# Graph layers: masks of the first stage written in place over the signs and stored twice per graph

## The chip, the cores and the metric

One core of a Trainium2 chip runs the whole kernel. The metric is the device time of one execution, in microseconds; lower is better. TensorE, VectorE (DVE in the rows), ScalarE (ACT), GpSimd (POOL) and SyncE (SP) each have their own queue of instructions, worked off in order, and are tied together by semaphores. All transfers are issued from SyncE's queue.

## What is computed

There are 16 graphs of 1024 nodes with 128 features and a dense weighted adjacency `adj` (about 6% of it not zero). Cut to what matters:

```python
h = relu(layernorm(x))
x = x + L0(h, adj)        # three times: h = h @ W + b; cos of the rows; (adj * cos) @ h
h = relu(layernorm(x))
keep = dilate(adj > 0)    # row by row, in order: removes neighbours by rank,
                          # each removal is made in row n and in column n
adj_d = adj * keep
x = x + L1(h, adj_d)      # three SAGE layers with batch norm over all 16 graphs,
                          # then a linear layer over the three outputs
```

`keep` depends on `adj` alone. For a graph it is the matrix R of what each row keeps, times its transpose: an edge stays where both ends keep it.

## The kernel before

The kernel has three stages: `layer0`, `layer1_middle` (twice over the graphs) and `layer1_last`. The change is in `layer0`, with its consequences for the loads of the mask in `layer1_middle`.

**Two programs in one stage.** `layer0` runs two things at once. The units (`plan_units`) are the 48 pairs of graph and layer of L0, with 16 steps each, 768 in all: TensorE makes a block of cosines (`cos`, lines 712 to 714), VectorE multiplies it by the adjacency into `ew` (line 895), and TensorE multiplies that by `Hr` (`agg`, line 721). `nh` and `nl` (lines 801 and 887) are the normed features at the beginning of a unit; the cosines of a unit can't begin before them. The dilation (`plan_dilation`) works on quads of four graphs, two quads at a time, block by block of 128 rows (k = 0 to 7). For a block, the rows of `adj` are loaded (`row`, three buffers `af`), ScalarE writes their signs into `Ab` as fp8 (line 815), a DMA transpose brings them into the slab `TT` (`fill`), VectorE strikes what earlier blocks removed (`low`, lines 911 and 915), GpSimd masks a triangle (line 641) for VectorE's `cross` (line 925), and rounds of `rank`, `rule` and `drop` follow. Then TensorE, ScalarE (`v`, line 832) and VectorE (`wide`, line 1010) write the kept row block into `TT`. `check` compares the last two rounds and reads the diagonal block in `TT`.

**The slab.** `TT[slot, m, k, x, s]` holds for one graph column block 2m + s and row block k, the two columns of a pair beside each other, one byte each. There are eight slots: quads 0 and 1, then quads 2 and 3 in the same ones.

**Masks.** When enough row blocks are done, a flip (m, j), a DMA transpose of column pair m and row blocks 4j to 4j + 3, is put into one of four flip buffers. With it VectorE makes `mask(q, j)` (line 1022) for row blocks q = 2m and 2m + 1: half a row block, 128 x 512 bytes, R times its transpose. It goes to one of three buffers `kp`, and from there SyncE stores it in `S["keep"]` (line 618), 64 KB each, 256 in all. Before the next mask can use the buffer, VectorE waits for the semaphore `kps` of that store. Flips (0,0) and (1,0) can go from k = 3, (2,0) from k = 5, and (3,0), (0,1), (1,1), (2,1), (3,1) from k = 7: 2, 1 and 5 for each graph. They are ordered by (m, j), and within it by graph.

**The order.** A planner in Python (`Planner.order`) lays all steps of both programs out beforehand, by list scheduling with fixed costs and ranks (a lower rank goes first among steps ready at the same time: `cos` 0, `mask` 3, `wide` 4, `low` and `cross` 5, `check` 6). Each engine then runs its list in that order, whatever really happens. Rings of buffers (`kp` 3, `flip` 4, `af` 3, `v` 3) are part of the plan. An issue on SyncE is counted as 70 ns, a flip's transfer as 600 ns, a mask's store as 300, and 100 ns for a signal between engines.

**Later stages.** `layer1_middle` loads the mask of a graph, 1 MB, as 8 rows of 1 KB for each partition, and multiplies the adjacency by it in eight instructions of 128 x 1024: all on VectorE in the first pass (line 1632), half on VectorE (line 1713) and half on GpSimd (line 1735) in the second.

Of the kernel before, what the change touches and what calls it, by code (L numbers as in the profile page):

```python
# [17 lines left out]
G = 16  # L18
N = 1024
D = 128  # L20
NK = 8
BANK = 76
# [13 lines left out]
RANKS = 3 * NK + 2  # L36
FLIPS = [(0, 0), (1, 0), (2, 0), (3, 0), (0, 1), (1, 1), (2, 1), (3, 1)]
# [20 lines left out]
def flat2(t):  # L58
    return t[:].rearrange("p k d -> p (k d)")

# [44 lines left out]
def build(nc, A):  # L105
    with ExitStack() as top:
# [17 lines left out]
        S["keep"] = nc.dram_tensor("scr_keep", [G, NK, 128, N], U8, kind="Internal").ap()  # L124
# [5 lines left out]
        C["kp0"] = C["stage"][:, 0:4, :].rearrange("p a b -> p (a b)").bitcast(FP8).rearrange("p (k n) -> p k n", k=NK)  # L130
# [173 lines left out]
def readers(quad, i, k):  # L304
    seen = [(q, k // 4) for q in range(NK)] + [(k, 1 - k // 4)]
    return [("dve", "mask", quad, i, q, j) for q, j in seen]
# [94 lines left out]
def plan_dilation(P):  # L401
# [3 lines left out]
    for n in sorted(range(QUADS * NK), key=lambda n: (n // NK // 2 * NK + n % NK, n // NK % 2)):  # L405
# [7 lines left out]
        for i in range(Q):  # L413
            freed = readers(quad - 2, i, k) if quad > 1 else []
# [42 lines left out]
def layer0_plan():  # L457
# [10 lines left out]
               [("dma", "mask", quad, i, q, j) for q in range(NK) for j in range(2)] + [("act", "row", n, i, j) for n in range(NK * QUADS) for i in range(Q) for j in range(2)])  # L468
    return P.order({"D0": 1, "D1": 1, "af": 3, "v": 3, "kp": 3, "flip": 4}), P.turns["kp"]


def layer0(nc, A, C, S):
    with ExitStack() as ctx:
# [3 lines left out]
        T = P.sems("at0 at1 fl0 fl1 fl2 fl3 af0 af1 af2 sign low au x bs b0 b1 ct ru vr sd again v8 wb wd av rw kp kps0 kps1 kps2 sum tot flag")  # L477
# [29 lines left out]
        kp = [P.sb(f"kp{i}", [128, 512], FP8) for i in range(3)]  # L507
# [6 lines left out]
        plan, ring = layer0_plan()  # L514
# [22 lines left out]
        def in_pairs(half_row):  # L537
            return half_row.rearrange("p (m x s) -> p m s x", m=2, s=2)

        def as_blocks(half_row):  # L540
            return half_row.rearrange("p (m s x) -> p m s x", m=2, s=2)

# [9 lines left out]
        every = [("dve", "mask") + a for a in ring]  # L552
# [8 lines left out]
        def sp(e):  # L561
# [3 lines left out]
            for kind, *a in plan["sp"]:  # L565
# [24 lines left out]
                elif kind == "fill":  # L590
# [4 lines left out]
                    if quad > 1:  # L595
                        wait_masks(e, readers(quad - 2, i, k))
                    e.dma_start_transpose(TT[:, slot, :, k].rearrange("p m x s -> p m (x s)").bitcast(F16),
                                          Ab[:, slot, :].bitcast(F16)).then_inc(T[f"at{quad % 2}"], 16)
                elif kind == "flip":
                    quad, i, m, j = a  # L600
                    r = nth["sp", "flip", quad, i, m, j] - 1
                    e.wait_ge(T["rw"], max(nth["dve", "wide", quad * NK + b, i, m // 2] for b in range(4 * j, 4 * j + 4)))
                    if r > 3:
                        wait_masks(e, users_of(*of["sp", "flip"][r - 4]))
# [1466 lines left out]
```

## Time and profile before

| | us |
|---|---|
| median of 3 runs | 2692.42 |
| lowest and highest | 2684.85 and 2693.45 |
| the profiled execution, its own time | 2686.08 |
| its span, first to last instruction | 2684.3 |
| TensorE busy | 2574.4 |
| VectorE busy | 2082.9 |
| ScalarE busy | 1365.9 |
| GpSimd busy | 598.8 |

The times below are from the start of the span of the profiled execution, which is 1.8 us shorter than its time. In it the first stage takes some 1630 us. A busy time of TensorE is that of instructions in flight: matmuls overlap, and their ends are modelled. "Idle before" is the time in which an engine had nothing to run, put down to what released it.

### The profile page before, as it was taken

What the parts mean: (1) busy time and instruction counts of PE and PEld (TensorE: products, weight loads), DVE (VectorE), ACT (ScalarE), POOL (GpSimd) and SP (SyncE); (2) the same over time, 40 slices, a digit from 0 to 9 for tenths busy, and PEclk for the clock granted to TensorE, in tenths of its full rate; (3) what the DMA queues carried; (4) which work ended last, traced back from release to release, by engine and by line L of the source; (5) the groups of instructions that cost most, each with busy time, mean ns of one, the idle gap of its engine ahead of it and who ended that gap; (6) DMA issues with size and microseconds to landing.
All of it is one profiled execution on the core that took longest, in us unless ns stands there. A gap on an engine that the chain in (4) does not pass through costs nothing. (4 is left out here: it accounts for less than half of the span.)

```text
span 2684.3 us, 38830 instructions
## 1 busy us (share of the span) xinstructions
PE 2574.4 (96%) x12390; PEld 1634.7 (61%) x12390; DVE 2082.9 (78%) x5413; ACT 1365.9 (51%) x4060; POOL 598.8 (22%) x265
## 2 busy tenths in 40 slices
PE   6999989999989999999999998999999999999898
PEld 4666656656655666656665664555555555555797
DVE  5788889889889988989989877766666635666676
ACT  4566645665654676646663421332322344443676
POOL 0000000000000000000000003766666603433673
PEclk8999999999999999999999999999999999999999
DMA  7254184364177347157345223555555419996663
GB/s 246 79 164 132 48 201 136 97 158 155 43 197 194 89 146 192 49 157 198 93 113 159 46 69 137 201 192 192 192 191 191 183 55 387 405 404 261 251 234 152
DMA packets 325878, 455.48 MB, mean 170 GB/s; under 512 B 155680, under 2 KB 218528, under 8 KB 325664
## 3 DMA queue, kind: packets, MB, share of 16 engines
q1 hardware_dynamic: 325664, 452.89, 52.4%
q8 instruction: 102, 1.67, 0.3%
q14 instruction: 112, 0.92, 0.1%
HBM read 352.13 MB, written 67.11 MB: 156 GB/s over the span
## 5 line engine op out<-in xcount | busy, mean ns | idle before, releaser
L721 PE MATMUL a_acc<-a_ew,a_Hr 128*128 128x512 f32 x1536 | 754.4, 600 | 0.0
L895 DVE TENSOR_TENSOR a_ew<-adj,a_cos 128x512 f32<-128x512 f32 x768 | 508.0, 681 | 69.0 <-PE a_cos L714 67.1
L712 PE MATMUL a_cos<-a_nh 128*128 128x512 f32 x768 | 417.2, 543 | 31.5 <-DVE a_ew L895 16.4
L721 PEld LDWEIGHTS a_acc<-a_ew,a_Hr 128*128 128x128 f32 x1536 | 275.8, 190 | 153.7 <-issue 110.2
L641 POOL TENSOR_TENSOR a_Au<-a_Ab,tri 128x512 fp8e4<-128x512 fp8e4 x32 | 36.8, 1150 | 1367.2 <-ACT a_Ab L815 1367.2
L832 ACT ACTIVATE a_v<-a_D,a_wb,a_small 128x256 f16<-128x256 f32 x512 | 287.2, 632 | 99.8 <-PE a_D L754 59.9
L714 PE MATMUL a_cos<-a_nh,a_nl 128*128 128x512 f32 x768 | 305.5, 398 | 0.0
L713 PE MATMUL a_cos<-a_nl,a_nh 128*128 128x512 f32 x768 | 302.9, 394 | 0.0
L822 ACT ACTIVATE a_vr<-a_D,a_small 128x128 f16<-128x128 f32 x432 | 161.9, 457 | 134.1 <-DVE a_small L967 133.8
L1387 PE MATMUL b_acc<-adj,b_z 128*128 128x512 f32 x512 | 225.0, 592 | 0.0
L712 PEld LDWEIGHTS a_cos<-a_nh 128*128 128x128 f32 x768 | 146.1, 190 | 127.5 <-DVE a_ew L895 52.7
L1484 PE MATMUL b_acc<-adj,b_z 128*128 128x512 f32 x512 | 222.5, 592 | 0.0
L1724 POOL TENSOR_TENSOR b_dsum<-adj 128x1024 f32<-128x1024 f32 x15 | 133.3, 8886 | 387.8 <-DVE adj L1632 387.8
L1728 POOL TENSOR_TENSOR b_dsum<-b_dsum,adj 128x1024 f32<-128x1024 f32 x90 | 211.5, 2350 | 12.9
L1022 DVE TENSOR_TENSOR a_kp<-a_T,stage 128x512 fp8e4<-128x512 fp8e4 x256 | 171.5, 688 | 47.2 <-DMA scr_keep<-a_kp 42.3
L815 ACT ACTIVATE a_Ab<-stage 128x512 fp8e4<-128x512 f32 x256 | 155.8, 630 | 99.7 <-DMA stage<-in_adj 98.9
L1010 DVE SCALAR_TENSOR_TENSOR a_T<-a_v,a_Ab 128x512 fp8e4<-128x512 f16 x256 | 173.1, 686 | 28.6 <-ACT a_v L832 28.2
L713 PEld LDWEIGHTS a_cos<-a_nl,a_nh 128*128 128x128 f32 x768 | 147.0, 191 | 64.3 <-issue 51.7
L714 PEld LDWEIGHTS a_cos<-a_nh,a_nl 128*128 128x128 f32 x768 | 145.4, 189 | 33.9
L1484 PEld LDWEIGHTS b_acc<-adj,b_z 128*128 128x128 f32 x512 | 96.0, 190 | 114.3 <-issue 112.2
L1387 PEld LDWEIGHTS b_acc<-adj,b_z 128*128 128x128 f32 x512 | 94.8, 190 | 107.1 <-issue 107.1
L784 ACT ACTIVATE h<-a_Hr 128x128 f32<-128x128 f32 x384 | 113.1, 297 | 78.3 <-DVE a_Hr L875 78.2
(267 smaller groups left out, 4361.3 us busy)
## 6 DMA issues: line engine op xcount, KB each, us to landing
adj<-in_adjT SPq DMA_DIRECT2D x108, 1024.0 KB, 12.6
adj<-in_adjT SPq DMA_DIRECT2D x128, 512.0 KB, 4.0
stage<-in_adj SPq DMA_DIRECT2D x256, 256.0 KB, 3.3
scr_keep<-a_kp SPq DMA_DIRECT2D x256, 64.0 KB, 1.8
scr_z<-b_zT SPq DMA_DIRECT2D x32, 512.0 KB, 3.7
scr_ag<-b_a SPq DMA_DIRECT2D x32, 512.0 KB, 3.3
stage<-scr_keep SPq DMA_DIRECT2D x13, 1024.0 KB, 7.3
b_kp<-scr_keep SPq DMA_DIRECT2D x12, 1024.0 KB, 7.8
```

Source lines behind the costliest of these rows:

```text
L712: e.matmul(cos[j][:], n[:, blk(k)], n[:, half(j)], start=True, stop=False)
L713: e.matmul(cos[j][:], n[:, blk(k)], m[:, half(j)], start=False, stop=False)
L714: e.matmul(cos[j][:], m[:, blk(k)], n[:, half(j)], start=False, stop=True).then_inc(E["cos"], 1)
L721: e.matmul(acc[j][:], Hr[u % 2][:, k, :], ew[idx % EW][:], start=(k == 0), stop=(k == NK - 1)).then_inc(E["agg"], 1)
L822: e.activation(vr[p][:, i, :], D0[:, i, :], ACT.Abs, bias=sm[p]["b2"][:, i:i + 1], scale=sm[p]["sc"][:, i:i + 1]).then_inc(T["vr"], 1)
L832: t = e.activation(v[c % 3][:, g * 256:g * 256 + 256].rearrange("p (x s) -> p s x", s=2), D1[:, 2 * g:2 * g + 2, :], ACT.Abs, bias=wb[p][: ...
L895: e.tensor_tensor(ew[idx % EW][:], adj[g % 2][:, k, half(j)], cos[j][:], ALU.mult).then_inc(E["ew"], 1)
L1010: e.scalar_tensor_tensor(TT[:, slot, 2 * j:2 * j + 2, k].rearrange("p m x s -> p m (x s)"), v[c % 3][:].rearrange("p (m c) -> p m c", m=2) ...
L1022: e.tensor_tensor(as_blocks(kp[c % 3][:]), row_half(slot, j, q), turned[:, :, :, :, q % 2], ALU.mult, saturate=False).then_inc(T["kp"], 1)
L1387: t = e.matmul(acc[j][:], src[:, q, :], adj[n % 3][:, q, half(j)], start=(q == 0), stop=(q == NK - 1))
L1484: t = e.matmul(acc[j][:], z[m % 2][:, q, :], adj[slot(m)][:, q, half(j)], start=(q == 0), stop=(q == NK - 1))
L1728: e.tensor_tensor(d, d, b[:, q, :], ALU.add).then_inc(E["ds"], 1)
```

## The change

The mask is written over R itself, in `TT`, instead of into a ring of `kp` buffers. When all 16 masks of a graph are made, its slab is stored by two transfers of 512 KB, in the slab's own layout, so 32 stores instead of 256. `S["keep"]` is now `[G, 128, NK * N]`; later stages load it as one piece of 8 KB for each partition and read it with steps that undo the layout (`masked`). `dilate_all`, which runs only when a check fails, writes the same layout.

Since masks overwrite what flips and `check` read, there are new waits. A mask (q, j) waits for all flips that read its block, as far as they are released by then (`flips_ahead`); a flip waits for masks already made in the blocks that it reads (`masks_ahead`); the mask that holds the diagonal block waits for `check` of its row block. A fill of quads 2 and 3 waits for both stores of the graph that had the slot. The order of the flips is changed: all of one graph, then the next graph. The constant `MASK` is 3, the rank that masks had before.

```diff
+def released(m, j):
+    return max(2 * m + 1, 4 * j + 3)
+def crossing(q, j):
+    return [(m, q // 4) for m in (2 * j, 2 * j + 1)]
+def flips_ahead(q, j):
+    return [f for f in crossing(q, j) if released(*f) <= released(q // 2, j)]
+def masks_ahead(m, j):
+    return [(q, h) for q in range(NK) for h in range(2)
+            if (m, j) in crossing(q, h) and released(q // 2, h) < released(m, j)]
 ...
-            freed = readers(quad - 2, i, k) if quad > 1 else []
+            freed = [("dma", "store", quad - 2, i, j) for j in range(2)] if quad > 1 else []
 ...
-        for m, j in FLIPS:
-            if k == max(2 * m + 1, 4 * j + 3):
-                for i in graphs_of(quad):
+        for i in graphs_of(quad):
+            for m, j in FLIPS:
+                if k == released(m, j):
                     transfer(("flip", quad, i, m, j), 600, [("dve", "wide", quad * NK + b, i, m // 2)
-                             for b in range(4 * j, 4 * j + 4)], "flip", "flip", rank=2)
+                             for b in range(4 * j, 4 * j + 4)] + [("dve", "mask", quad, i) + a for a in masks_ahead(m, j)],
+                             "flip", "flip", rank=2)
+            for m, j in FLIPS:
+                if k == released(m, j):
                     for q in (2 * m, 2 * m + 1):
                         last = ("flip", ("flip", quad, i, m, j)) if q % 2 else None
-                        add("dve", ("mask", quad, i, q, j), 605, 3, [("dma", "flip", quad, i, m, j),
-                            ("dve", "wide", quad * NK + q, i, j)], f"flip{quad}{i}{m}{j}", "kp", last)
-                        transfer(("mask", quad, i, q, j), 300, [("dve", "mask", quad, i, q, j)], None, None, "kp")
+                        add("dve", ("mask", quad, i, q, j), 605, MASK, [("dma", "flip", quad, i, m, j),
+                            ("dve", "wide", quad * NK + q, i, j)] + ([("dve", "check", quad * NK + q)] if j == q // 4 else [])
+                            + [("dma", "flip", quad, i) + f for f in flips_ahead(q, j)], f"flip{quad}{i}{m}{j}", None, last)
+            if k == NK - 1:
+                for j in range(2):
+                    transfer(("store", quad, i, j), 1400, [("dve", "mask", quad, i, q, j) for q in range(NK)])
 ...
                     if quad > 1:
-                        wait_masks(e, readers(quad - 2, i, k))
+                        e.wait_ge(T[f"st{i}"], 32 * (quad - 1))
 ...
-                elif kind == "mask":
-                    quad, i, q, j = a
-                    c = ring[quad, i, q, j]
-                    wait_masks(e, [("dve", "mask", quad, i, q, j)])
-                    e.dma_start(S["keep"][quad * Q + i, q][:, half(j)], kp[c % 3][:].bitcast(U8)).then_inc(
-                        T[f"kps{c % 3}"], 16)
+                elif kind == "store":
+                    quad, i, j = a
+                    slot = Q * (quad % 2) + i
+                    wait_masks(e, [("dve", "mask", quad, i, q, j) for q in range(NK)])
+                    if quad and j == 0:
+                        e.wait_ge(T[f"st{i}"], 32 * quad)
+                    e.dma_start(S["keep"][quad * Q + i][:, 4096 * j:4096 * j + 4096],
+                                TT[:, slot, 2 * j:2 * j + 2].rearrange("p m k x s -> p (m k x s)").bitcast(U8)).then_inc(
+                        T[f"st{i}"], 16)
 ...
-                    if c > 2:
-                        e.wait_ge(T[f"kps{c % 3}"], 16 * (c // 3))
+                    if j == q // 4:
+                        e.wait_ge(T["v8"], nth["dve", "check", quad * NK + q])
+                    mine = row_half(slot, j, q)
                     turned = flip[r % 4].bitcast(FP8).rearrange("p (m t) (x s) -> p m t x s", t=2, s=2)
-                    e.tensor_tensor(as_blocks(kp[c % 3][:]), row_half(slot, j, q), turned[:, :, :, :, q % 2], ALU.mult,
-                                    saturate=False).then_inc(T["kp"], 1)
+                    e.tensor_tensor(mine, mine, turned[:, :, :, :, q % 2], ALU.mult, saturate=False).then_inc(T["kp"], 1)
 ...
+        def masked(b, c, q):
+            row = b[:, q, :].rearrange("p (m s x) -> p m s x", s=2, x=128)
+            return row, row, c.rearrange("p (m k x s) -> p m k s x", m=4, k=NK, s=2)[:, :, q]
 ...
-                e.dma_start(kp[n % 2].bitcast(U8), S["keep"][ORDER[n]].rearrange("k p n -> p k n")).then_inc(
+                e.dma_start(kp[n % 2].bitcast(U8), S["keep"][ORDER[n]]).then_inc(
 ...
-                    e.tensor_tensor(b[:, q, :], b[:, q, :], c[:, q, :], ALU.mult).then_inc(E["mk"], 1)
+                    e.tensor_tensor(*masked(b, c, q), ALU.mult).then_inc(E["mk"], 1)
```

## Rows read from the trace of the kernel before

**Rows 1.** The page, part 1: busy time, share and instructions of each engine.

```profile
PE 2574.4 (96%) x12390; PEld 1634.7 (61%) x12390; DVE 2082.9 (78%) x5413; ACT 1365.9 (51%) x4060; POOL 598.8 (22%) x265
```

**Rows 2.** Stretches: length, PE, PEld, DVE, ACT, POOL busy, clock, DMA; two sums.

```profile
60.00:340.00 280.00, 277.65 (x1467) 180.87 (x1467) 227.61 (x655) 180.30 (x502) 6.59 (x6) 1.00 0.37 106
...
sum 1560.00, PE 1503.13 PEld 962.33 DVE 1356.98 ACT 898.63 POOL 34.60; mean PE 107.37 PEld 68.74 DVE 96.93 ACT 64.19 POOL 2.47
...
720.00:900.00 180.00, 164.70 (x801) 102.17 (x799) 162.65 (x379) 97.42 (x259) 4.79 (x4) 1.00 0.70 174
...
sum 540.00, PE 495.33 PEld 312.14 DVE 478.96 ACT 254.39 POOL 12.80; mean PE 82.56 PEld 52.02 DVE 79.83 ACT 42.40 POOL 2.13
...
1700.00:1800.00 100.00, 100.00 (x377) 56.09 (x376) 64.12 (x147) 30.74 (x98) 69.89 (x22) 1.00 0.52 194
```

**Rows 3.** Stretches of L895 (two), of L1022 (sum of the six); L1022's durations, first and last.

```profile
60.00:340.00 280.00, 92.50 (x138) 1.00 0.37 106
...
720.00:900.00 180.00, 52.70 (x82) 1.00 0.70 174
...
sum 540.00, DVE 140.42; mean DVE 23.40
...
L1022 DVE TENSOR_TENSOR a_kp<-a_T,stage x256: 636/685/1418, 335.0 to 1573.3; 128x512 fp8e4<-128x512 fp8e4 x128
```

**Rows 4.** Waits of the first stage: engine, line, what released it; total, times, longest.

```profile
PE a_cos L712 <- DVE a_nl L887: 12.4, 9, 3.0
PE a_D L754 <- ACT a_v L832: 11.5, 14, 2.3
...
ACT a_Ab L815 <- DMA stage<-in_adj: 98.9, 67, 5.9
DVE a_kp L1022 <- DMA scr_keep<-a_kp: 42.3, 49, 2.3
DVE a_kp L1022 <- DMA stage<-a_T: 1.8, 1, 1.8
```

**Rows 5.** The same waits from 720 to 900 us alone.

```profile
ACT a_Ab L815 <- DMA stage<-in_adj: 24.3, 14, 4.0
DVE a_kp L1022 <- DMA scr_keep<-a_kp: 15.6, 19, 2.1
```

**Rows 6.** Timeline: start, duration, instruction; a mask that waits for a store.

```profile
740.29 1.19 SPq L597 DMA_TRANSPOSE a_T<-a_Ab  x1
...
741.52 0.59 SPq L618 DMA_DIRECT2D scr_keep<-a_kp  x1
...
742.93 0.69 DVE L1022 TENSOR_TENSOR a_kp<-a_T,stage 128x512 fp8e4<-128x512 fp8e4 x1 [2.15 <-DMA scr_keep<-a_kp]
```

**Rows 7.** Timeline: a late row, and TensorE's wait 5 us after.

```profile
1067.63 0.63 ACT L815 ACTIVATE a_Ab<-stage 128x512 fp8e4<-128x512 f32 x1 [2.75 <-DMA stage<-in_adj]
...
1072.62 0.80 PE L712 MATMUL a_cos<-a_nh 128*128 128x512 f32 x1 [3.03 <-DVE a_nl L887]
```

**Rows 8.** Store issues (ns, min/median/max); transfers: KB each, median us to landing.

```profile
L618 SPq DMA_DIRECT2D scr_keep<-a_kp x256: 332/431/1826, 335.8 to 1574.0; - x128
...
stage<-scr_keep SPq DMA_DIRECT2D x13, 1024.0 KB, 7.3
...
scr_x<-xt SPq DMA_DIRECT2D x16, 512.0 KB, 2.7
...
stage<-a_T SPq DMA_TRANSPOSE x128, 2.5
```

**Rows 9.** Groups by form: count, busy us, mean ns, idle before: mask, `low`, triangle, later products.

```profile
L1022 DVE TENSOR_TENSOR a_kp<-a_T,stage 128x512 fp8e4<-128x512 fp8e4 x256 | 171.5, 688 | 47.2 <-DMA scr_keep<-a_kp 42.3 <-DMA stage<-a_T 1.8
...
L641 POOL TENSOR_TENSOR a_Au<-a_Ab,tri 128x512 fp8e4<-128x512 fp8e4 x32 | 36.8, 1150 | 1367.2 <-ACT a_Ab L815 1367.2
...
L1735 POOL TENSOR_TENSOR adj<-adj,stage 128x1024 f32<-128x1024 f32 x20 | 39.6, 2012 | 121.4 <-DMA adj<-in_adjT 121.4
...
L911 DVE TENSOR_TENSOR a_T<-a_T 128x512 fp8e4<-128x512 fp8e4 x32 | 22.1, 694 | 0.0
```

More of the change, by code:

```diff
@@ L21 @@
 NK = 8
-BANK = 76
+BANK = 77
 MAGIC = 8388608.0
@@ L467, in layer0_plan @@
                                        for i in range(Q) for q in range(NK) for j in range(2)] +
-               [("dma", "mask", quad, i, q, j) for q in range(NK) for j in range(2)] + [("act", "row", n, i, j) for n in range(NK * QUADS) for i in range(Q) for j in range(2)])
-    return P.order({"D0": 1, "D1": 1, "af": 3, "v": 3, "kp": 3, "flip": 4}), P.turns["kp"]
+               [("dma", "store", quad, i, j) for j in range(2)] + [("act", "row", n, i, j) for n in range(NK * QUADS) for i in range(Q) for j in range(2)])
+    return P.order({"D0": 1, "D1": 1, "af": 3, "v": 3, "flip": 4})
 def layer0(nc, A, C, S):
@@ L476, in layer0 @@
                    "bst bag lnsd lnrs lnr " + " ".join(f"adj{i}{k}" for i in range(2) for k in range(NK)))
-        T = P.sems("at0 at1 fl0 fl1 fl2 fl3 af0 af1 af2 sign low au x bs b0 b1 ct ru vr sd again v8 wb wd av rw kp kps0 kps1 kps2 sum tot flag")
+        T = P.sems("at0 at1 fl0 fl1 fl2 fl3 af0 af1 af2 sign low au x bs b0 b1 ct ru vr sd again v8 wb wd av rw kp st0 st1 st2 st3 sum tot flag")
         W, rows = P.sb("W", [128, 3, 128]), P.sb("rows", [128, 3, 128])
@@ L513, in layer0 @@
         mv4 = C["mv"][:].rearrange("p (g k) -> p g k", k=NK)
-        plan, ring = layer0_plan()
+        plan = layer0_plan()
         nth = {}
@@ L550, in users_of @@
             return [("dve", "mask", quad, i, q, j) for q in (2 * m, 2 * m + 1)]
-        every = [("dve", "mask") + a for a in ring]
+        every = [("dve", "mask") + a for a in of["dve", "mask"]]
         def earlier(engine, kind, upto):
@@ L602, in sp @@
                     e.wait_ge(T["rw"], max(nth["dve", "wide", quad * NK + b, i, m // 2] for b in range(4 * j, 4 * j + 4)))
+                    ahead = [("dve", "mask", quad, i) + a for a in masks_ahead(m, j)]
                     if r > 3:
-                        wait_masks(e, users_of(*of["sp", "flip"][r - 4]))
+                        ahead += users_of(*of["sp", "flip"][r - 4])
+                    if ahead:
+                        wait_masks(e, ahead)
                     e.dma_start_transpose(flip[r % 4], TT[:, Q * (quad % 2) + i, m, 4 * j:4 * j + 4].rearrange(
@@ L623, in sp @@
                     wait_masks(e, every)
-                    stored = [ring[quad, i, q, j] for q in range(NK) for j in range(2)]
-                    for c in range(3):
-                        e.wait_ge(T[f"kps{c}"], max(16 * (m // 3 + 1) for m in stored if m % 3 == c))
-                    e.dma_start(C["kp0"].bitcast(U8), S["keep"][ORDER[0]].rearrange("k p n -> p k n")).then_inc(
-                        C["kpload"], 16)
+                    e.wait_ge(T[f"st{i}"], 32 * (quad + 1))
+                    e.dma_start(C["kp0"].bitcast(U8), S["keep"][ORDER[0]]).then_inc(C["kpload"], 16)
             e.wait_ge(E["xs"], 16 * (G - 1))
-            for c in range(3):
-                e.wait_ge(T[f"kps{c}"], 16 * ((2 * G * NK + 2 - c) // 3))
+            for i in range(Q):
+                e.wait_ge(T[f"st{i}"], 32 * QUADS)
         def pool(e):
@@ L1193, in dve @@
                         e.wait_ge(E["tr"], j + 1)
[L1194 to L1195 removed]
+                        for m in range(2):
+                            into = kp[:, 512 * j + 256 * m:512 * j + 256 * m + 256].rearrange("p (x s) -> p s x", s=2)
+                            turned = Dp[:, j, 256 * m:256 * m + 256].rearrange("p (s x) -> p s x", s=2)
+                            mine = R[:, q, 512 * j + 256 * m:512 * j + 256 * m + 256].rearrange("p (s x) -> p s x", s=2)
+                            t = e.scalar_tensor_tensor(into, turned, 0.5, mine, ALU.is_lt, ALU.is_gt, saturate=False)
+                        t.then_inc(E["kp"], 1)
                 def sp(e):
                     e.wait_ge(E["kp"], 2)
[L1199 to L1200 removed]
+                    e.dma_start(graph(S["keep"]).rearrange("o p (m k c) -> (o p) m k c", k=NK, c=256)[:, :, q],
+                                kp[:].bitcast(U8).rearrange("p (m c) -> p m c", c=256)).then_inc(E["load"], 16)
                     e.wait_ge(E["load"], 16)
```

37 lines of the change are left out of this document (15 added, 22 removed).

## The prediction

> **What bounds the kernel now.** I read the page first, for the shares. TensorE is busy 96% of the span, and VectorE in places nearly as much [rows 1]. Such a share doesn't say whether TensorE waits, so next came the busy times by stretch. The first stage ends near 1630 us. From 60 to 1620 us TensorE is idle 57 us in all (1560 less the 1503.13 of the first sum line), and this idle time isn't spread evenly [rows 2]. Six stretches, 340 to 440, 720 to 900, 1040 to 1080, 1140 to 1180, 1400 to 1480 and 1480 to 1580, hold 540 less 495.33 = 44.7 us of it (the second sum line), and 140.42 us of the mask products, at 688 ns each some 205 of the 256, lie in them [rows 3, 9]. The largest, 720 to 900, has 15.3 us. The 280 us from 60 to 340, without masks, have 2.3.
>
> The second measure is the pace of the `ew` product, one for each of the 768 steps of the first stage: 138 in 280 us from 60 to 340, 82 in 180 us from 720 to 900 [rows 3], so 2.03 against 2.20 us for a step. TensorE's work, not VectorE, is therefore the floor, and what can be won is idle time in the mask stretches.
>
> What ends the idle time is in the waits [rows 4]. VectorE waits 42.3 us for `kps`, the landing of a mask's store from the ring of three buffers. TensorE's own waits are for `ew`, for `nl` (12.4 us), and for ScalarE's `v` (11.5 us). ScalarE waits 98.9 us for the rows that SyncE loads. In 720 to 900 alone these are 15.6 us (VectorE, stores) and 24.3 us (ScalarE, rows) [rows 5]. The timeline shows how they hang together [rows 6]: the mask of 742.93 was kept back 2.15 us, and the store whose buffer it needed went out only at 741.52, since SyncE was busy with the transpose of 740.29. SyncE's queue is full in such places, with transposes of 1.19 us and stores of 0.59 us. The planner that wrote the order counts 70 ns for each issue, so it can't see this. Further on, the chain reaches TensorE [rows 7]: a row late by 2.75 us, then the triangle product, VectorE's `cross` and, behind it in the queue, `nl`, and TensorE starts the next unit after 3.03 us of idleness.
>
> **The change, part by part.** *Stores.* 256 stores of 64 KB become 32 of 512 KB. Each issue takes a median of 431 ns [rows 8], so SyncE is relieved of 224 x 0.431 = 97 us, nearly all in the mask stretches. The bytes stay the same. VectorE's ring wait goes: 42.3 us [rows 4], nearly all in the six stretches and 15.6 of it in the longest [rows 5]. What is late next is the flip transpose, below.
>
> *The mask itself* writes bytes two apart instead of side by side. The trace has the same size written this way, in place: 694 ns for `low` against 688 for the mask [rows 9]. 256 x 6 ns = 1.5 us. Two more waits stand ahead of some masks, on semaphores mostly long reached; back-to-back instructions with three waits already follow each other without idle time, so I take nothing, at most 1.5 us.
>
> *The flips.* Before, a mask needed one flip. Now it also needs those that read the blocks it overwrites. At k = 7 a graph has five flips and ten masks; the first mask (6,0) needs flips (3,0), (0,1), (1,1), and the masks of (2,1) need (3,1). The fifth flip takes the ring slot of the first, so it waits for (7,0). One flip takes SyncE 1.19 us, and lands 2.5 us after its issue [rows 8]. Between the graphs: the next graph's third flip gets its slot when (5,1) of this graph is done. Only masks (6,1) and (7,1), 1.2 to 1.4 us, and one or two `ew` products of about 0.6 us stand between, against 2.5 to 3.7 us for issue and landing. Left over are 0 to 2.5 us; I take 1.5, for 16 graphs 24 us. The bounds: nothing, if VectorE has dilation work planned there (then the latency hides behind it), and 16 x 3.7 = 59 us if nothing covers it. At k = 3 and k = 5 at most two flips are needed and they go out together; included in that. What queues behind a waiting mask is `ew`, so this is the very place where the 42.3 us hurt. Behind a waiting flip on SyncE stand row loads and fills; but before, 256 stores waited there for masks in the same way, and now 32 do, so the queue is freer on balance.
>
> *Fills.* A fill of graphs 8 to 15 now waits for both stores of the graph two quads before. The nearest row, a 512 KB store to scratch, lands in 2.7 us [rows 8]. Two in a row, before the first fill of two quads: 0 to 6 us for each quad, on the chain of the dilation, not on TensorE. The last mask starts at 1573 [rows 3] and the stage ends near 1630, so up to 50 us of such delay is covered by the last units; without that cover it would cost its full 12 us. By the Trainium skill ("DMA: Bandwidth & Descriptors", Anatomy of one DMA) a transfer costs about 2.0 us plus its bytes at 436 GB/s, an estimate of 3.2 us for such a store; the trace has 2.7, and either is covered.
>
> *Later stages.* The loads of the masks keep their 1 MB, in pieces of 8 KB instead of 1 KB. They land in 7.3 us now [rows 8], and nobody waits for them: TensorE is busy 100% from 1700 on [rows 2]. VectorE's and GpSimd's mask products now read bytes two apart. For VectorE the 694 against 688 says nothing changes. GpSimd takes 2012 ns; the nearest row is the triangle product, which reads bytes two apart: 1150 ns for 512 [rows 9], so up to 2.3 us for 1024, 4 x 0.3 us for a graph. In that stage GpSimd waits for the loads of the adjacency itself, so its work has room; I take nothing, and at most 3 us, for the last graph and its neighbours. By the Trainium skill ("GPSIMD Engine Reference", Performance pitfalls for Q7 kernels) reads slow by half from a step above 8 bytes. The step here is 2, so by the rule GpSimd's time stays; no run yet shows it.
>
> **The sum.** VectorE's idle time changes by -42.3 + 24 + 1.5 = -17 us. What a microsecond of it is worth to TensorE: in the six stretches 44.7 us of idleness stand beside 42.3 us of ring waits, but part of it comes from late rows. I take 0.6, so -10 us. The freed SyncE brings rows earlier: of its 57 us TensorE waits 11.5 for `v` and 12.4 for `nl` [rows 4], which hang on ScalarE and so on the rows; I take a quarter of these 24, -6 us. Sum: -16 us. The static order, which the planner shuffles with every edit, can add or take some microseconds; I give it no sign. The profiled execution took 2686.08 us; 2670 would follow from it. The median of the runs shown, 2692.42, is 6.3 above it, so the runs give 2676.
>
> **Rivals.** (a) *The flips take the place of the stores.* The wait for each graph is 3.7 us, uncovered: 59 us in place of 42.3, plus 1.5. VectorE idles 18 us more, at the worth of 0.6 TensorE loses 11 us, and the freed SyncE does not help, since it waits itself: 2703. It decides against the change from 42.3 / 16 = 2.6 us of waiting per graph on. For it: the planner counts 770 ns (70 for the issue, 600 for the transfer, 100 for the signal) for what takes 2.5 to 3.7, and at k = 7 the masks come one every 2 us. Against it: in the trace only one wait of 1.8 us was for a flip [rows 4]. The Trainium skill has the rule behind it ("DMA: Bandwidth & Descriptors", Rules for kernel authors): issue a DMA early and wait late; three flips ahead of a mask instead of one brings the wait nearer. (b) *Nothing shows.* The ring wait was slack of VectorE, TensorE's idleness comes from the coupling of units and dilation, and the new order keeps it: 2692, 2684 to 2700. For it: in the wait at 742.93 TensorE had matmuls to do. (c) *All of it comes back.* Flips are covered and SyncE was the cause of nearly all: -41 us of TensorE's 44.7, 2650. For it: only 2.3 us of idleness in the 280 us without masks.
>
> **How the numbers follow.** Forecast 0.45, (c) 0.15, (b) 0.22, (a) 0.18. Within 0.3% is +-8 us, about what this measurement can tell from no change. The forecast's own range is 2665 to 2684; nine tenths of it and all of (c) are faster, (b) is mostly same. Faster 0.59, same 0.22, slower 0.19. The range that holds 8 in 10 reaches from 2652, close to (c), to 2703, where (a) stands.
>
> **What the profile would show.** Right: no wait of a mask for a store; the mask product still near 690 ns; 32 stores; in the mask stretches TensorE idle 25 us instead of 45; waits of masks for flips of 10 to 40 us, most at k = 7; ScalarE's wait for rows below 80 us; from 1700 on no difference. Wrong: flip waits above 42 us, or TensorE's idle time unmoved though VectorE's ring waits are gone, or the last mask later than the end of the units.

## The result, and the profile after

| us | before | after |
|---|---|---|
| median of 4 runs | 2690.78 | 2657.26 |
| lowest and highest | 2684.85 and 2693.45 | 2653.77 and 2661.80 |
| the profiled execution, its own time | 2686.08 | 2658.54 |
| its span | 2684.3 | 2656.7 |

The ratio is 0.9879, with a 95% interval of 0.9856 to 0.9903: the kernel is 33.5 us faster, twice the 16 us of the forecast. The page after, part 1:

```profile
PE 2568.9 (97%) x12390; PEld 1636.7 (62%) x12390; DVE 2079.9 (78%) x5413; ACT 1365.2 (51%) x4060; POOL 606.5 (23%) x265
```

The counts are those of [rows 1], and the busy times nearly so. What went is idle time, and it went in the first stage: the last `agg` of the units, and the first instruction of the middle stage (a constant `onesf` that VectorE writes), before and then after, by tile (duration min/median/max, first and last start):

```profile
L721 PE MATMUL a_acc<-a_ew,a_Hr x1536: 590/592/1057, 34.1 to 1620.3; 128*128 128x512 f32 x192
...
L1648 DVE MEMSET onesf<- x1: 165/165/165, 1630.0 to 1630.0; 128x128 f32 x1
```

```profile
L745 PE MATMUL a_acc<-a_ew,a_Hr x1536: 590/592/1057, 34.1 to 1590.8; 128*128 128x512 f32 x192
...
L1680 DVE MEMSET onesf<- x1: 165/165/165, 1600.5 to 1600.5; 128x128 f32 x1
```

The first stage is 29.5 us shorter. The stages behind it take 1.9 us more (2656.7 - 1600.5 = 1056.2 against 2684.3 - 1630.0 = 1054.3). So the two profiled executions differ by 27.6 us, and the medians by 33.5: the profiled execution before lies 4.7 us under its median, that after 1.3 us above. In which stage the other 5.9 us lie, no trace shows. The stretches of the kernel after, with that of the `ew` product (line 919) in 720 to 900 and the sum of the prediction's six mask stretches:

```profile
60.00:340.00 280.00, 277.08 (x1463) 180.08 (x1464) 226.85 (x654) 179.54 (x499) 6.73 (x6) 1.00 0.36 106
340.00:440.00 100.00, 94.26 (x461) 60.92 (x460) 92.18 (x240) 45.72 (x124) 2.20 (x2) 0.98 0.64 182
720.00:900.00 180.00, 169.64 (x829) 107.42 (x828) 160.73 (x362) 87.78 (x253) 5.37 (x4) 1.00 0.73 191
...
720.00:900.00 180.00, 56.24 (x86) 1.00 0.73 191
...
sum 540.00, PE 521.35 PEld 332.88 DVE 486.64 ACT 263.86 POOL 7.57; mean PE 86.89 PEld 55.48 DVE 81.11 ACT 43.98 POOL 1.26
...
60.00:1590.00 1530.00, 1494.98 (x7540) 961.24 (x7541) 1349.59 (x3655) 897.65 (x2500) 35.96 (x30) 1.00 0.45 129
```

Up to the end of the units TensorE is now idle 1530 - 1494.98 = 35.0 us, 22 less than the 57 of [rows 2]. Without masks, 60 to 340, nothing changed (2.9 against 2.3 us). In 720 to 900 idleness fell from 15.3 to 10.4 us, and 86 `ew` products run there instead of the 82 of [rows 3]. The six stretches together have 540 - 521.35 = 18.7 us of it, and 188 of the 256 masks lie in them. The other 7.6 us of the 29.5 are not in TensorE's idle column; matmuls in flight overlap, so this column need not hold all of its waiting.

The waits of the first stage: TensorE's for `ew` before, which [rows 4] leaves out, and then those after, which answer to [rows 4]:

```profile
PE a_cos L712 <- DVE a_ew L895: 16.4, 16, 2.1
```

```profile
ACT a_Ab L839 <- DMA stage<-in_adj: 88.4, 61, 8.1
...
PE a_D L778 <- ACT a_v L856: 11.8, 17, 1.9
...
DVE a_T L1048 <- issue: 10.8, 7, 3.5
...
DVE a_T L1048 <- DMA stage<-a_T: 7.0, 6, 1.5
PE a_cos L736 <- DVE a_nl L911: 6.4, 6, 2.4
PE a_cos L736 <- DVE a_ew L919: 5.8, 8, 1.3
```

The wait for stores is gone. Masks wait 17.8 us for flips: 7.0 us by name, and 10.8 put down to "issue", where no semaphore event of the profile ends the wait. TensorE's wait for `ew` fell from 16.4 to 5.8. Its wait for `nl` fell from 14.8 to 6.4, both counted from the stage's start (the 12.4 of [rows 4] leave out the first 60 us, and without these it is 4.0 after). That for `v` is as it was. ScalarE's wait for rows fell only from 98.9 to 88.4. The products by form, and the transfers of the page:

```profile
L1048 DVE TENSOR_TENSOR a_T<-a_T,stage 128x512 fp8e4<-128x512 fp8e4 x256 | 168.1, 692 | 19.7 <-issue 10.8 <-DMA stage<-a_T 7.0 <-DVE a_X L1028 0.9
L1767 POOL TENSOR_TENSOR adj<-adj,stage 128x1024 f32<-128x1024 f32 x20 | 42.0, 2132 | 121.1 <-DMA adj<-in_adjT 121.1
```

```profile
scr_keep<-a_T SPq DMA_DIRECT2D x32, 512.0 KB, 3.2
...
stage<-scr_keep SPq DMA_DIRECT2D x13, 1024.0 KB, 6.8
```

A mask takes 692 ns against 688 [rows 9]; there are 32 stores, and the loads of the later stages land no later than in [rows 8].

### The profile page after: what moved, and what is told of

The parts are those of the page before. It is cut to its first block and busy times, and to the rows that moved or that the text cites. A ratio compares the mean times of both kernels' runs of the same rounds, so it can differ in the third digit from the quotient of the medians.

```text
span 2656.7 us, 38841 instructions
## 1 busy us (share of the span) xinstructions
PE 2568.9 (97%) x12390; PEld 1636.7 (62%) x12390; DVE 2079.9 (78%) x5413; ACT 1365.2 (51%) x4060; POOL 606.5 (23%) x265
## 5 line engine op out<-in xcount | busy, mean ns | idle before, releaser
L736 PE MATMUL a_cos<-a_nh 128*128 128x512 f32 x768 | 421.2, 548 | 12.4 <-DVE a_nl L911 6.4
L839 ACT ACTIVATE a_Ab<-stage 128x512 fp8e4<-128x512 f32 x256 | 155.8, 631 | 88.7 <-DMA stage<-in_adj 88.4
L1048 DVE TENSOR_TENSOR a_T<-a_T,stage 128x512 fp8e4<-128x512 fp8e4 x256 | 168.1, 692 | 19.7 <-issue 10.8
## 6 DMA issues: line engine op xcount, KB each, us to landing
adj<-in_adjT SPq DMA_DIRECT2D x108, 1024.0 KB, 12.7
```

Source lines behind the costliest of these rows:

```text
L736: e.matmul(cos[j][:], n[:, blk(k)], n[:, half(j)], start=True, stop=False)
L1048: e.tensor_tensor(mine, mine, turned[:, :, :, :, q % 2], ALU.mult, saturate=False).then_inc(T["kp"], 1)
```

## The experiments

Three questions: is it the stores on SyncE, the ring wait, or the planner's new order? And how much does an order change the time by itself? Every kernel's profile was read at the same four places, and the table has them, each from that kernel's own profiled execution: the last mask's start (the end of the dilation), the last `agg`'s start (the end of the units), the start of the middle stage, and TensorE's wait there for the first masked block of the adjacency. "Before" is the median of the kernel before on the same chip. Runs with different medians of it were on different chips or at different times; differences between them, taken below from the medians, shift by up to 3 us if they are taken from the ratios.

| kernel | median | before | ratio, 95% | last mask | last agg | middle | wait |
|---|---|---|---|---|---|---|---|
| before | 2690.78 | | | 1573.3 | 1620.3 | 1630.0 | 8.7 |
| after | 2657.26 | 2690.78 | 0.9879, 0.9856 to 0.9903 | 1556.1 | 1590.8 | 1600.5 | 8.6 |
| e1 extra stores | 2689.32 | 2690.71 | 0.9995, 0.9985 to 1.0004 | 1587.4 | 1621.4 | 1631.0 | 8.5 |
| e2 with ring wait | 2733.09 | 2690.71 | 1.0166, 1.0137 to 1.0195 | 1630.5 | 1665.6 | 1675.2 | 8.6 |
| e3 before, by graph | 2691.88 | 2690.71 | 1.0003, 0.9992 to 1.0014 | 1625.3 | 1621.0 | 1634.5 | 12.4 |
| e4 old plan | 2675.31 | 2690.71 | 0.9936, 0.9918 to 0.9955 | 1606.6 | 1583.1 | 1615.8 | 31.6 |
| e5 tiny stores | 2687.61 | 2693.36 | 0.9982, 0.9971 to 0.9993 | 1586.2 | 1620.2 | 1629.9 | 8.7 |
| e6 no wait | 2689.04 | 2693.36 | 0.9987, 0.9978 to 0.9997 | 1587.3 | 1621.3 | 1630.9 | 8.5 |
| e7 old plan, stores | 2705.54 | 2693.36 | 1.0057, 1.0036 to 1.0078 | 1631.3 | 1601.0 | 1641.1 | 39.0 |
| e8 and ring wait | 2730.53 | 2693.36 | 1.0148, 1.0127 to 1.0168 | 1658.7 | 1621.7 | 1668.7 | 45.9 |
| e9 masks aside | 2670.55 | 2691.36 | 0.9934, 0.9918 to 0.9951 | 1573.7 | 1600.7 | 1610.3 | 8.5 |
| e10 aside, e8's rest | 2703.01 | 2691.36 | 1.0045, 1.0029 to 1.0062 | 1634.9 | 1627.0 | 1644.9 | 16.9 |
| e11 true costs | 2637.83 | 2691.36 | 0.9806, 0.9790 to 0.9822 | 1568.0 | 1562.0 | 1577.5 | 14.5 |
| e12 rows on ScalarE | 2662.10 | 2691.36 | 0.9888, 0.9871 to 0.9904 | 1562.0 | 1596.7 | 1606.3 | 8.5 |
| e13 before, signal | 2680.48 | 2693.22 | 0.9961, 0.9950 to 0.9971 | 1615.9 | 1611.1 | 1624.8 | 12.6 |
| e14 after, signal | 2687.27 | 2693.22 | 0.9981, 0.9970 to 0.9992 | 1619.2 | 1593.0 | 1628.8 | 34.6 |
| e15 before, true costs | 2655.19 | 2693.22 | 0.9867, 0.9847 to 0.9887 | 1561.4 | 1588.1 | 1597.8 | 8.6 |
| e16 e11, MASK 4 | 2649.79 | 2693.22 | 0.9853, 0.9834 to 0.9871 | 1581.8 | 1564.3 | 1591.0 | 25.6 |
| e17 before, both | 2640.47 | 2691.63 | 0.9797, 0.9774 to 0.9820 | 1575.5 | 1576.3 | 1585.9 | 8.5 |
| e18 after, both | 2671.15 | 2691.63 | 0.9918, 0.9898 to 0.9939 | 1601.0 | 1563.0 | 1610.3 | 46.2 |

In every row the middle stage begins some 9.7 us after the last `agg`, or 9 to 10 us after the last mask, whichever is later. So two chains end the stage, and the two columns say which of them did. In ten of the kernels (e3, e4, e7, e8, e10, e11, e13, e14, e16, e18) it was the dilation, and TensorE waits 12 to 46 us for the first block there, where it waits some 8.6 us otherwise.

**e1, e2 and e3: the stores and the ring wait, put back one by one; the order of the flips alone.** e1 keeps the instructions of after on all other engines and adds 256 stores of 64 KB of a constant on SyncE, each behind its mask; e2 adds a mask's wait for the store three masks ago.

```diff
+    timed = [(P.steps[("sp",) + name].begin, 0, name) for name in out["sp"]]
+    timed += [(s.end, 1, ("extra",) + s.name[1:]) for key, s in P.steps.items() if key[:2] == ("dve", "mask")]
+    out["sp"] = [name for _, _, name in sorted(timed, key=lambda t: t[:2])]
...
+                elif kind == "extra":
+                    wait_masks(e, [("dve", "mask", quad, i, q, j)])
+                    e.dma_start(S["dump"][quad * Q + i, q][:, half(j)], C["UL"][:].bitcast(U8)[:, 0:512]).then_inc(
+                        T[f"dump{c % 3}"], 16)
```

(Left out: the scratch tensor, three semaphores and the room for them, and a wait for all extra stores at the end of the stage.) Ahead of the mask, in e2 alone:

```diff
+                    if c > 2:
+                        e.wait_ge(T[f"dump{c % 3}"], 16 * (c // 3))
```

e3 is the kernel before with the loops over flips turned:

```diff
-        for m, j in FLIPS:
-            if k == max(2 * m + 1, 4 * j + 3):
-                for i in graphs_of(quad):
+        for i in graphs_of(quad):
+            for m, j in FLIPS:
+                if k == max(2 * m + 1, 4 * j + 3):
```

> The changed kernel with 256 more stores of 64 KB on SyncE, one behind each mask and waiting for it, of a constant to an unused scratch tensor; nobody waits for them before the end of the stage. Theory 1 (the gain of 33 us came from VectorE's ring wait): SyncE's 97 us of issues are slack, the time stays within 5 us of the changed kernel, 2652 to 2662. Theory 2 (it came from the freed queue of SyncE): 15 us or more come back, 2672 or above. Theory 3 (it came from the new order): no change, as in theory 1.

> As the run before, and each mask also waits for the landing of the extra store three masks ago, so the ring wait is back. Theory 1: 20 to 33 us above the run before, which means near 2685. Theory 2: at most 8 us above it. Theory 3: both runs stay below 2670, since the order of the changed kernel is kept.

> The kernel before with nothing changed but the order of flips and masks: all of one graph, then the next. Theory 1 and theory 2: the ring and the 256 stores are still there, so 2685 to 2700. Theory 3: below 2675.

e1 gives back 32.1 us, nearly all of the gain. e2 costs 43.8 us more, which none of the three theories had foretold, so the two together (76) are more than twice what the change brought. The order of the flips alone brings nothing. The extra stores of e1, and its waits of masks and rows:

```profile
L656 SPq DMA_DIRECT2D scr_dump<-UL x256: 319/430/1879, 338.8 to 1588.1; - x128
```

```profile
ACT a_Ab L852 <- DMA stage<-in_adj: 109.6, 58, 8.3
...
DVE a_T L1061 <- issue: 23.0, 12, 6.4
PE a_cos L749 <- DVE a_ew L932: 21.1, 23, 2.8
DVE a_T L1061 <- DMA stage<-a_T: 17.8, 13, 2.5
```

An issue takes 430 ns. Masks wait 40.8 us for flips in place of 17.8, and behind a waiting mask stands `ew`: TensorE waits 21.1 us for it, 5.8 in after. From 60 to 1621 us it is idle 57.6 us in e1, against 35.0 to the end of the units in after. SyncE's queue around 738 us in e1, and then in after, by timeline (start, duration, instruction):

```profile
736.12 1.05 SPq L656 DMA_DIRECT2D scr_dump<-UL  x2
737.28 1.19 SPq L634 DMA_TRANSPOSE stage<-a_T  x1
738.51 0.58 SPq L649 DMA_DIRECT2D scr_keep<-a_T  x1
739.13 1.86 SPq L656 DMA_DIRECT2D scr_dump<-UL  x3
741.47 1.19 SPq L623 DMA_TRANSPOSE a_T<-a_Ab  x1
742.71 0.58 SPq L656 DMA_DIRECT2D scr_dump<-UL  x1
743.38 2.50 SPq L634 DMA_TRANSPOSE stage<-a_T  x2
```

```profile
732.55 0.57 SPq L644 DMA_DIRECT2D scr_keep<-a_T  x1
735.46 1.19 SPq L618 DMA_TRANSPOSE a_T<-a_Ab  x1
737.17 2.51 SPq L629 DMA_TRANSPOSE stage<-a_T  x2
739.73 0.57 SPq L644 DMA_DIRECT2D scr_keep<-a_T  x1
```

In e1 the queue is free for 0.8 of these 9.8 us (the largest gap, 740.99 to 741.47, is 0.5 us), and a flip (L634) that is ready has to stand in line. In after, where the stores are missing, it is free for 2.9 of 7.7 us, with one gap of 2.3 us (733.12 to 735.46). No mask waits just here. The longest wait of one in e1 comes 50 us later; SyncE's queue, VectorE's and TensorE's, in order:

```profile
777.41 1.19 SPq L623 DMA_TRANSPOSE a_T<-a_Ab  x1
...
779.27 0.90 SPq L656 DMA_DIRECT2D scr_dump<-UL  x2
...
780.75 0.46 SPq L656 DMA_DIRECT2D scr_dump<-UL  x1
781.30 2.50 SPq L634 DMA_TRANSPOSE stage<-a_T  x2
...
786.22 1.30 DVE L1061 TENSOR_TENSOR a_T<-a_T,stage 128x512 fp8e4<-128x512 fp8e4 x2 [6.44 <-issue]
...
789.29 0.50 PE L749 MATMUL a_cos<-a_nh 128*128 128x512 f32 x1 [2.78 <-DVE a_ew L932]
```

SyncE issues without a break from 777.41 on, and the last of the two flips leaves its queue at 783.80. The mask starts 2.4 us after that, with `nl` and `ew` behind it, and TensorE stands still for 2.78 us. That this flip is what the mask waited for fits the 2.5 us of [rows 8], but the trace names no releaser.

The ring wait of e2, in a plan that doesn't know of it, is twice that of [rows 4], and costs half of its length:

```profile
DVE a_T L1064 <- DMA scr_dump<-UL: 84.0, 48, 5.2
```

**e4, e7 and e8: the old resources in the plan.** In e4 the planner still counts 256 stores and the ring of three, though neither exists; e7 issues the stores where they are planned (e1's), e8 adds the ring wait of e2.

```diff
-    + [("dma", "flip", quad, i) + f for f in flips_ahead(q, j)], f"flip{quad}{i}{m}{j}", None, last)
+    + [("dma", "flip", quad, i) + f for f in flips_ahead(q, j)], f"flip{quad}{i}{m}{j}", "kp", last)
+    transfer(("planned", quad, i, q, j), 300, [("dve", "mask", quad, i, q, j)], None, None, ("kp", ("mask", quad, i, q, j)))
...
-    return P.order({"D0": 1, "D1": 1, "af": 3, "v": 3, "flip": 4})
+    return P.order({"D0": 1, "D1": 1, "af": 3, "v": 3, "kp": 3, "flip": 4})
```

> The changed kernel, laid out by a planner that still counts 256 stores and a ring of three buffers for the masks; nothing of them is issued, so VectorE waits for no store and SyncE has 32 stores. Theories 1 and 2: within 8 us of the changed kernel, 2649 to 2665. Theory 3, in the form that a plan without the ring packs the work better: 15 us or more above it, 2672 or more.

> The changed kernel laid out for 256 stores and a ring of three (as in the fourth experiment), and now the 256 stores are really issued where the plan has them, of a constant; no mask waits for one. Theory 2 (SyncE's issues cost wherever they are): 15 to 30 us above the fourth experiment, 2690 to 2705. Theory 2 with a plan that has room for them: 2675 to 2682.

> As the run before, and each mask waits for the landing of the store three masks ago, as before the change. Theory 1 (the ring wait is worth 0.6 us of TensorE a us, 25 us): 2710 to 2730. Theory 2 alone (where SyncE is full the ring wait adds nothing of its own): within 8 us of the run before. In the first plan the ring added 44 us, with 84 us of waits; here the plan spaces the masks for the ring, so waits of 40 to 50 us are expected.

e4 has only 15.4 us of the gain. In it the units end 7.7 us earlier than in after, but the dilation ends 50 us later, and TensorE waits for it:

```profile
PE b_acc L1420 <- DVE adj L1665: 32.3, 2, 31.6
```

In this plan the stores cost 30.2 us again (e7 less e4, on two chips; 33 by the ratios), and the ring wait 25.0. So the price of the stores hardly depends on the plan in these two, while that of the ring wait does: with the ring in the plan masks wait 53.9 us for stores instead of 84.0. e8 has stores and ring wait again, and is still 37 us slower than the kernel before.

**e5 and e6: what of a store costs.** e5 is e1 with 8 bytes for each partition in place of 512; e6 is e1 without the stores' wait for masks.

```diff
-   e.dma_start(S["dump"][quad * Q + i, q][:, half(j)], C["UL"][:].bitcast(U8)[:, 0:512]).then_inc(
+   e.dma_start(S["dump"][quad * Q + i, q][:, 512 * j:512 * j + 8], C["UL"][:].bitcast(U8)[:, 0:8]).then_inc(
```

```diff
-   wait_masks(e, [("dve", "mask", quad, i, q, j)])
```

> The changed kernel with 256 extra stores as in the first experiment (SyncE, one behind each mask, waiting for it), but of 8 bytes per partition, 1 KB in all instead of 64. Theory 2a (the issue on SyncE costs): the time is that of the first experiment, 2685 to 2693. Theory 2b (the bytes on the DMA engines cost): it is that of the changed kernel, 2652 to 2664.

> The same 256 stores of 64 KB at the same places of SyncE's list, not waiting for the masks. Theory 2a (issue time on SyncE, about 110 us of it): 2680 or above. Theory 2c (each store ties SyncE to VectorE, so that it can't run ahead with rows and transposes): below 2668.

Neither the bytes nor the waiting: by the ratios e5 is 0.13% below e1 and e6 0.08%, at most 3.5 us of the 32. The issues of e5 take what those of e1 took:

```profile
L656 SPq DMA_DIRECT2D scr_dump<-UL x256: 319/430/1840, 338.7 to 1586.9; - x128
```

256 x 0.43 = 110 us of SyncE's time in its crowded stretches cost some 30 us.

**e9 and e10: masks not in place.** The masks go to three side buffers, and the waits that writing in place needs leave the code and the plan, that for `check` too. The 32 stores take the slab without masks, so these two kernels leave the masks out of what later stages read. e10 has this with the plan, the stores and the ring wait of e8.

```diff
-    for b in range(4 * j, 4 * j + 4)] + [("dve", "mask", quad, i) + a for a in masks_ahead(m, j)],
+    for b in range(4 * j, 4 * j + 4)],
...
-    e.tensor_tensor(mine, mine, turned[:, :, :, :, q % 2], ALU.mult, saturate=False).then_inc(T["kp"], 1)
+    e.tensor_tensor(as_blocks(side[(nth["dve", "mask", quad, i, q, j] - 1) % 3][:]), mine, turned[:, :, :, :, q % 2], ALU.mult, saturate=False).then_inc(T["kp"], 1)
```

> The changed kernel with the masks written beside the slab, into three small buffers that nobody stores; the 32 stores take the slab as it is, without masks. So the extra waits of in-place writing (masks for the flips that read their block, masks for check, flips for earlier masks) go from the code and from the plan; stores, their number and the fills' wait for them stay. Theory 4 (in-place writing has a price of its own, which the gain of 33 us is already net of): 10 to 35 us below the changed kernel, 2622 to 2647. Rival: the waits are covered, within 8 us of it, 2649 to 2665.

> The plan, the 256 extra stores and the ring wait of the eighth experiment, but masks beside the slab as in the run before. This is nearly the kernel before, with 32 stores more. Theory 4: 25 us or more below the eighth experiment, 2690 to 2705. Rival: what lies between the eighth experiment and the kernel before (39 us) is the 32 stores and the fills that wait for them, and it stays at 2720 to 2735.

e9 has fewer constraints and is 13 us slower than after; e10 is 27.5 us faster than e8, as the theory of a price of in-place writing had it. The same edit has either sign. My theory that the waits of the in-place masks are a cost which the gain has to pay fell in e9 for the written plan. Since a mask's median duration is the same there (685 ns), I put the 13 us down to the plan, which is an argument and was not tested by itself.

**e11 and e12: act on the cause.** e11 lets the planner count what an issue on SyncE takes; e12 takes the 256 row loads from SyncE's queue and issues them from ScalarE's, in the order of after's plan.

```diff
-        self.add("sp", name, 70, rank, after, chain, takes)
+        self.add("sp", name, 1200 if name[0] in ("fill", "flip") else 500, rank, after, chain, takes)
```

```diff
+    timed = [(P.steps[("act",) + name].begin, 1, name) for name in out["act"]]
+    timed += [(P.steps[("sp",) + name].begin, 0, ("load",) + name[1:]) for name in out["sp"] if name[0] == "row"]
+    out["act"] = [name for _, _, name in sorted(timed, key=lambda t: t[:2])]
+    out["sp"] = [name for name in out["sp"] if name[0] != "row"]
```

> The changed kernel, with a planner that counts an issue on SyncE as 1200 ns for a transpose and 500 ns for any other transfer, in place of 70. Theory 2 (SyncE's issue time is the hidden resource, and the list is laid out in ignorance of it): 5 to 20 us below the changed kernel, 2637 to 2652. Rival: the list on each engine is already near enough, within 5 us.

> The changed kernel, with the 256 loads of rows of the adjacency issued from ScalarE's queue instead of SyncE's, at the places that the plan gives them. Theory 2: SyncE is freed of another 110 us or more of issues; if its queue still limits the mask stretches, 5 to 20 us below the changed kernel, if it doesn't any more, no change. ScalarE is busy half of the time; if an issue holds it for 0.4 us ahead of work that TensorE waits for, the time goes above 2665.

e11 is the best version here: 2637.83 us, 19.4 us under after and 53.5 under before. Its waits for rows and flips:

```profile
ACT a_Ab L839 <- DMA stage<-in_adj: 48.3, 38, 5.6
...
DVE a_T L1048 <- DMA stage<-a_T: 3.1, 3, 1.3
```

e12 brings ScalarE's wait for rows down to 38.0 us, further than e11, and gains nothing (0.9888 against 0.9879 for after). So a shorter wait for rows does not by itself bring TensorE time, and my forecast had counted on that. e12 also takes 256 x 0.432 = 111 us of issues off SyncE's queue, as many as the stores, and still gains nothing. Either that queue no longer limits this plan, or the issues cost as much on ScalarE, where they take a median of 334 ns each, 86 us in all:

```profile
L800 ACTq DMA_DIRECT2D stage<-in_adj x256: 334/334/1550, 5.6 to 1371.2; - x128
```

For a cost in their new place, or of the order, speaks that masks wait 23.3 us for flips in e12 (17.8 in after) and TensorE 11.3 us for `ew` (5.8). Which of the two it is was not tested.

**e13 to e18: the same change under other plans.** e13 and e14 are the two kernels with a signal counted as 130 ns instead of 100; e15 is before with the true costs of e11; e17 and e18 have both; e16 is e11 with the constant `MASK` 4 instead of 3.

```diff
-SIGNAL = 100
+SIGNAL = 130
```

> The kernel before, with the planner's cost of a signal between engines at 130 ns instead of 100. Nothing else changes, and no price of any step; the list on each engine comes out in another order. If a plan's luck is worth less than 5 us: 2686 to 2697. If it is worth 10 us and more, then part of the 33 us can be luck.

> The changed kernel with the same edit of the planner, 130 ns for a signal. Without luck in the plan: 2652 to 2663, and 30 to 36 us below the run before. With luck: farther off, in either direction.

> The kernel before, with a planner that counts SyncE's issues as 1200 and 500 ns, as in the eleventh experiment. Theory 2: the plan then spaces masks and stores by what SyncE can issue; 5 to 25 us below the kernel before, 2666 to 2686, and the 256 stores still cost something, so 15 us or more above the eleventh experiment. If the change's gain came from the ignorance of the plan alone, this kernel reaches the eleventh one, within 8 us of 2638.

> The eleventh experiment with MASK = 4, so masks give way to rule and drop. In the eleventh the last mask starts at 1568 us and the stage ends 9 us later, so the dilation sets the stage's end. If masks in front of the chain of rounds are what makes it late: below 2634. Rival: the masks themselves end last, and pushed back they make it longer, above 2642.

> The kernel before, planned with SyncE's issues at 1200 and 500 ns and a signal at 130 ns. Against 2655 for the same at 100 ns: within 8 us if a plan that knows SyncE's issues has little luck in it, farther off if luck stays.

> The changed kernel, planned in the same way. Against 2638 at 100 ns: within 8 us if there is little luck in such plans. If the change itself, apart from the plan's luck, is worth 14 to 17 us, this is 10 to 22 us below the run before; if the end of the dilation sets the stage's end here, with a wait of TensorE above 20 us in the middle stage's beginning, less.

One assumed number, 100 or 130 ns for a signal, makes the kernel before 12.7 us faster (e13) and the kernel after some 30 us slower (e14). Counted issues make before 38 us faster (e15, against 5 to 25 expected), and they take away most of the wait that the change was to remove, 16.8 us in place of 42.3:

```profile
DVE a_kp L1022 <- DMA scr_keep<-a_kp: 16.8, 21, 1.9
```

A later rank for the masks only moves the dilation's end 14 us back, and e16 is 12 us slower than e11. e17, the kernel before with both, reaches 2640.47 without the change, as good as e11.

The change, after less before, under four pairs of plans:

| plan | time | last agg | last mask | middle stage begins |
|---|---|---|---|---|
| as written | -33.5 | -29.5 | -17.2 | -29.5 |
| signal 130 | +6.8 | -18.1 | +3.3 | +4.0 |
| true costs (two chips) | -17.4 | -26.1 | +6.6 | -20.3 |
| both | +30.7 | -13.3 | +25.5 | +24.4 |

The time follows the start of the middle stage, within 7 us: the times are of medians, the starts of single executions. The units end earlier in all four, by 22 us on the mean; the dilation ends later in three. In these three the changed kernel's dilation ends after its units, and the gain shrinks to 17 us (true costs) or turns into a loss (signal 130, both). TensorE's wait for it in e18:

```profile
PE b_acc L1419 <- DVE adj L1664: 46.2, 1, 46.2
```

## Why the prediction was right and wrong

The sign was right, and 2657 lies in the range, but the size was off by a factor of two. By its steps:

- **The ring wait, -42.3 us of VectorE's idle time at a worth of 0.6.** The wait is gone. Its worth was measured at 0.5 (84.0 us of waits for 43.8 us, e2), near the 0.6, in a plan that doesn't expect it; in one that does it is 25 us of time for 53.9 us of waits (e8 less e7), 0.5 again.
- **The flip waits, +24.** Measured 17.8, in the 10 to 40 foretold. Rival (a) did not come. Its main ground was false: I read the planner as counting 770 ns for a flip, and it also adds a tail of 2000 ns to each transfer and 100 ns for each of two signals, 70 + 100 + 600 + 2000 + 100 = 2870 ns, against 2.5 us from issue to landing [rows 8].
- **The freed SyncE, -6: the term that failed.** Putting the 256 issues back into the plan of after costs 32 us, and 30 in the old plan. I had counted 97 us off the queue rightly (431 ns each, and 430 again in e1), and then valued them by a quarter of TensorE's waits for `v` and `nl`. In e1 against after the chain goes another way: an issue delays the next flip, the flip a mask, the mask the `ew` behind it on VectorE (40.8 against 17.8 us of waits for flips, 21.1 against 5.8 us of TensorE for `ew`). In the kernel before masks waited 1.8 us for flips [rows 4], so there the full queue must have shown elsewhere, in part in the ring wait, whose store could itself be late in the queue [rows 6]. The two terms of my sum were thus not apart, and no run removes one of them from the kernel before. ScalarE's row wait, on which the term stood, fell to 88.4 us only, not below 80, and rose in 720 to 900 from 24.3 [rows 5] to 30.5; in e12 it fell by half with no gain.
- **The order, given no sign and "some microseconds".** This was far too little. The same change is worth from -33.5 to +30.7 us over four pairs of plans. On the path from before to after, 15.4 us come with the old resources in the plan (e4) and 18.1 with the plan that drops them (after less e4). That the stores cost 30 us and the ring wait 25 to 44, together more than the 33.5 measured, says that something of after is worse than in before; in e14 and e18 it is the end of the dilation, in the written plan it stays open. What part of the 33.5 us is this order's luck can't be read from four pairs. Their mean is -3 us. So that 2657 lies within the range is in part luck: the freed queue was worth some 26 us more than I gave it, and what is worse in the new order took a part of that back.
- **The dilation's delay, covered up to 50 us.** In the written plan so: 47 us of slack between last mask and last `agg` became 35. In the plans of e13 and e14 the dilation was last already, and there its delay costs in full. The cover belonged to one plan, not to the kernel. The fills waited 15.2 us in all for the slab's stores (7 times, at most 4.0), near the 12 foretold.
- **Rivals (b) and (c).** Something did show, against (b). (c) has the nearest time, 2650, and was right in that SyncE's queue carries most of it; but it had 41 us of TensorE's idleness come back, and 22 did.
- **The mask itself, +1.5 us.** 692 against 688 ns: 256 x 4 = 1.0 us. Right.
- **TensorE idle 25 instead of 45 us in the mask stretches.** In these stretches it is 18.7, and from 60 us to the end of the units it fell from 57 to 35, 22 us less: the direction was right and the size near, but it was not the whole gain. Another 7.6 us of the stage came without showing in the idle column.
- **Later stages, nothing to 3 us.** +1.9 us. GpSimd's mask product takes 2132 ns against 2012. By the Trainium skill ("GPSIMD Engine Reference", Performance pitfalls for Q7 kernels) a step of two bytes is below the one from which reads slow by half. The trace agrees in that there is no such slowing (2132 ns), though it has these 6%. That the 1.9 us are these 120 ns wasn't tested.

**What stays open.** Why the dilation ends so much later under a signal of 130 ns, in after above all, was not followed further; nor why e9, with fewer constraints, is slower than after. That both come from the order is argued by exclusion: e13 and e14 differ from their kernels in one number of the planner alone, e9 also in its code. What e12 would gain if its issues cost nothing on ScalarE is open too.

## What to carry to other kernels

Where a planner lays out the order, count what an issue takes on its queue: at 1200 and 500 ns instead of 70 both kernels got faster, by 38 us before (e15) and 19 after (e11), more than the change itself under that plan (17 us). With a signal of 130 ns it was 40 us before (e17 less e13) and 16 after (e18 less e14). Judge a change of such a kernel under several plans with a harmless cost shifted, and look at the end of each of its chains rather than at the time alone: a gain on one is worth only what the other leaves. A busy issuing queue was dear here through what stands behind it, and the largest wait that the page shows beside it, ScalarE's for rows, was not where it hurt.

## What the runs showed of the hardware

An issue on SyncE takes a median of 430 ns for a copy of 128 partitions, whether 64 KB (e1) or 1 KB (e5), and the flip transpose 1.2 us (1.19 in the timelines of e1 and after). The row load of 256 KB took a median of 432 ns of SyncE's queue in after and 334 of ScalarE's in e12. GpSimd's product of 128 x 1024 floats by fp8 took 2008 to 2014 ns in the five kernels with the masks side by side (before, e3, e13, e15, e17), and 2129 to 2136 ns in the fifteen with them two bytes apart, 6% more; VectorE's product of the same shape and steps stayed at 1213 ns after against 1216 before (first pass). GpSimd's triangle product, the same in all of them, varied from 1105 (e8) to 1202 ns (e11) from kernel to kernel.
